# Attention inner loop of a fused transformer kernel: the product with the values split in two halves of queries, and reordered between score products and row maxima

## Chip, core and metric

The kernel runs on one NeuronCore of a Trainium2 chip. The metric is the device time of one launch in microseconds (us): lower is better. The engines have short names here: PE is TensorE's matmul stream, PEld its weight loads, DVE is VectorE, ACT is ScalarE, POOL is GpSimd, SP is SyncE, which issues DMAs.

## What is computed

Four blocks in a row, each followed by a residual sum and a layer norm: a linear state-space scan, a mixture of eight experts with the top two taken, a multi-head attention and a feed-forward block with fp4-style rounding. Only the attention is touched. It runs over 4 sequences of 1024 tokens, 16 heads of 16 channels:

```
qkv = (zn @ W_qkv + b_qkv).reshape(b, n, 3, H, DH)
scores = jnp.einsum('bhqd,bhkd->bhqk', q, k) * scale
attn = jax.nn.softmax(scores, axis=-1)
msa = jnp.einsum('bhqk,bhkd->bhqd', attn, v)
...
out = msa_cat @ W_proj + b_proj
```

## The kernel before

The order of the work is written out by hand for each engine, and engines meet through counting semaphores, which the code calls flows. `F["ex"].wait(pe, b, n)` makes PE wait until flow `ex` has counted n in sequence b. An engine takes its instructions in order, so whatever is behind a waiting one waits too.

Heads are worked in pairs, p = 0 to 7, two heads (a = 0 and 1) at once: head 0 of the pair lies in rows 0 to 49 of `Qs` and `Ks`, head 1 in rows 64 to 113. Each pair has two kinds of score product.

- **Row maxima** (`score_max`, line 925; DVE line 1418). To find the largest score of each query, PE makes 32 products a pair, "units", of 128 queries by 512 keys, alternately of head 0 and head 1, each into a PSUM bank of its own. In the main loop there are three such banks (4, 5 and 6), used in turn, so a unit may start once DVE has reduced the unit three before it (flow `sld`). One DVE instruction reduces one unit.
- **Transposed scores** (`transposed_scores`, line 955). The same scores with keys in the partitions, and with the negated maximum added as two more rows (50 rows instead of 48). Two products, one for each head, give 128 keys by 512 queries. ACT takes the exponential of both in one instruction (line 676) from banks 0 and 1, or 2 and 3, into the buffer `Pb`.

The values are then weighed (`weigh`, line 968): for each head and half of the queries one product of 128 keys, 32 columns of V (16 channels and a column of ones for the softmax sum) and 512 queries, each into 32 partitions of bank 7. The four go to four groups of 32 columns of the array, and run side by side. These operands are plain fp32, and one such product is two MATMUL instructions in the trace, each with a load of its own.

The main loop goes over 64 steps m for each sequence. Step m has the transposed scores of pair p = m // 8 and key tile kt = m % 8, for both halves of the queries (qh = 0, 1), the weighing of step m - 1, and four units of the pair ahead: they run 12 units (three steps) ahead of the pair (`LEAD = 12`), so the last 11 steps of a sequence have none. The units of a pair done, DVE negates the maxima (lines 1422 to 1424, "negation" below), PE turns them (line 932) in the next step, DVE copies them (line 1431), and POOL issues four DMAs (line 497), one behind the other, that bring them into the two extra rows of `Qs`. PE waits for these (flow `mrow`) ahead of the first transposed score of the pair. When a pair is weighed, ACT copies bank 7 out (`evac_o`, line 643); PE waits for that copy (flow `ov`) before it weighs the first tile of the next pair.

Of the kernel before, what the change touches and what calls it, by code (L numbers as in the profile page):

```python
# [14 lines left out]
P = 128  # L15
B, S, D = 4, 1024, 256
N = 16
TT = S // P
DC = D // P
HALF = 512  # L20
NH = S // HALF
E, HID = 8, 512
HC = HID // P
HEADS, DH = 16, 16
NP = HEADS // 2
NB = 4
CH = P // DH
KT = S // P
# [51 lines left out]
def transformer(nc, xT, state_cols, WtT, WbT, Wc4, WoT, Dv, bo, sel, Wg, W1, b1, W2, b2, rev,  # L80
                lnw_d, lnb_d, Wqkv, bqkv_d, Wproj, bproj, w_gate, w_up, w_down, ident_d, out):
    ctx = ExitStack()
    with ctx:
# [150 lines left out]
        def h_dram(name, shape):  # L234
# [25 lines left out]
            ve=1, rs=2, nm=1, vel=2, rsl=4, nml=2, zn=TT, xn=1, xw=TT, xa=TT - 2 + TT // 2, xd=2 + TT // 2, x2=1, vm=1, trp=4 + 2, xt=4 + 2, xl=TT - 3,  # L260
            qkp=8, qka=8, qkv=8, vp=TT, vv=TT, **{f"stk{k}": NP // NB * STK for k in range(NB)}, mrow=16 * 4 * NP,
            slp=SLOTS, sld=SLOTS, nms=NP,
            bp=2 * KT * NP, ex=2 * KT * NP, pv=KT * NP, ov=NP,
            op=TT // 2, on=TT, mp=TT, mt=TT, pr=TT, rr=TT,
            xq=2, xr=2, px=8, xm=2, xp=2, gup=TT, sg=TT, hh=TT, hq=TT, htp=TT, htv=TT, dp=TT, dr=TT,
            outd=16, xfree=1, ahead=0, chain=0,
# [278 lines left out]
        def _(act):  # L545
# [93 lines left out]
            def sequence(b, more):  # L639
                def evac_o(p):  # L640

                    F["pv"].wait(act, b, KT * (p + 1))
                    F["ov"].inc(act.activation(OP[:, p, :], PS[:, 7, :], ACT.Copy))

                def late_norm(i):
# [23 lines left out]
                for p in range(NP):  # L669
                    for kt in range(KT):  # L670
                        for qh in range(2):
                            n = 2 * (KT * p + kt) + qh
                            F["bp"].wait(act, b, n + 1)
                            if n >= 4:
                                F["pv"].wait(act, b, (n - 4) // 2 + 1)
                            F["ex"].inc(act.activation(Pb[:, kt % 2, 2 * qh:2 * qh + 2, :],  # L676
                                                       PS[:, 2 * qh:2 * qh + 2, :], ACT.Exp, scale=0.25))
                        if kt == 0 and p > 0:
                            evac_o(p - 1)
                evac_o(NP - 1)  # L680
                if more:
                    ahead_root(b, 1)
# [60 lines left out]
        def _(pe):  # L743
# [135 lines left out]
            with pe.Fori(0, B) as b:  # L879
# [13 lines left out]
                for u in range(8):  # L893
                    c, w, th = u // 4, (u % 4) // 2, u % 2
                    if u >= 4:
                        F["qkv"].wait(pe, b, u - 3)
                    for kc in range(DC):
                        if w:
                            tokens = XT[:, kc, th * HALF:(th + 1) * HALF].rearrange("p (i q) -> p i q", q=P)
                        else:  # L900
                            tokens = XT[:, kc, :].rearrange("p (i h q) -> p h i q", h=2, q=P)[:, th, :, :]
                        ins = pe.matmul(PS[:, u % 4, :].rearrange("p (i q) -> p i q", q=P),  # L902
                                        wqkv[:, kc, w * D + c * P:w * D + (c + 1) * P], tokens,
                                        start=(kc == 0), stop=(kc == DC - 1))
                    F["qkp"].inc(ins)
                def values(t):
# [30 lines left out]
                def maxima(upto):  # L937

                    while issued[0] < min(upto, NP * UN):
                        n = issued[0]  # L940
                        if n >= UN + 4 and n % UN == 4:
                            turn_max(n // UN - 1)
                        score_max(n)
                        issued[0] += 1
                        if issued[0] == NP * UN:
                            turn_max(NP - 1)

                def transposed_scores(p, kt, qh):

                    n = 2 * (KT * p + kt) + qh  # L950
                    if n >= 2:
                        F["ex"].wait(pe, b, n - 1)
                    for a in range(2):
                        rows = slice(ROW * a, ROW * a + MROWS)
                        ins = pe.matmul(PS[:, 2 * qh + a, :], Ks[rows, p % NB, kt * P:(kt + 1) * P],  # L955
                                        Qs[rows, p % NB, qh * HALF:(qh + 1) * HALF], start=True, stop=True)
                    F["bp"].inc(ins)

                def weigh(m):

                    p, kt = m // KT, m % KT
                    if kt == 0 and p:
                        F["ov"].wait(pe, b, p)
                    F["ex"].wait(pe, b, 2 * m + 2)
                    for qh in range(2):
                        for a in range(2):
                            j = 2 * a + qh
                            ins = pe.matmul(PS[32 * j:32 * j + 32, 7, :], V[:, kt, 2 * p + a, :], Pb[:, kt % 2, 2 * qh + a, :],  # L968
                                            start=(kt == 0), stop=(kt == KT - 1), skip_group_check=True)
                    F["pv"].inc(ins)  # L970

                values(0)
# [8 lines left out]
                for m in range(NP * KT):  # L981
                    p, kt = m // KT, m % KT
                    if kt == 0:
                        F["mrow"].wait(pe, b, 16 * 4 * (p + 1))
                    ahead = UN + LEAD + 4 * m
                    transposed_scores(p, kt, 0)
                    maxima(ahead + 2)
                    transposed_scores(p, kt, 1)
                    maxima(ahead + 3)
                    if m:  # L990
                        weigh(m - 1)
                    maxima(ahead + 4)
                weigh(NP * KT - 1)

                F["ov"].wait(pe, b, NP)

# [607 lines left out]
```

How the kernel before makes its waits and increments, by code:

```python
    def wait(self, eng, b, n, ahead=0):  # L62
        eng.wait_ge(self.sem, b * self.per + (ahead * self.per + n))
# [12 lines left out]
    def wait(self, eng, n):  # L76
        eng.wait_ge(self.sem, n)
# [255 lines left out]
        @block.sync  # L333
# [62 lines left out]
                e_now = e_next  # L396
                if k >= 2:
                    store_y(k - 2)
                if k in (1, 4, 7):
                    for q in range(2):
                        C[f"mid{q}"].wait(sp, 16 * B // 2)
                    load_ffn(k // 3, (w_gate, w_up, w_down)[k // 3])
            store_y(TILES - 2)
            store_y(TILES - 1)
            sp.wait_ge(s_wev, len(turns))
            sp.wait_ge(s_one, 1)
            for k in range(NB):
                for a in range(2):
# [17 lines left out]
                                at = ROW * a + row * DH  # L427
                                F[f"stk{k}"].inc(sp.dma_start(dst[at:at + DH, k, :].bitcast(F32), lo if part else hi), by=16)
                F["xa"].wait(sp, b, TT - 2 + TT // 2)
                F["xd"].wait(sp, b, 2 + TT // 2)
                hold(sp, "sp")
                F["outd"].inc(sp.dma_start(out.rearrange("(n p) d -> p n d", p=P)[:, bass.ds(b * TT, TT), :],
                                           X[:, :, :]), by=16)
                F["outd"].wait(sp, b, 16)
                sp.sem_inc(F["xfree"].sem, 1)
                F["xfree"].seen += 1
            sp.wait_ge(F["outd"].sem, 16 * B)
# [2 lines left out]
        @block.gpsimd  # L440
# [98 lines left out]
                sequence(b, True)  # L539
            sequence(B - 1, False)
            pool.wait_ge(s_one, 1 + 16 * 2 * NB)
```

## Time and profile before

| | |
|---|---|
| time, median of 3 runs | 1864.62 us (1864.11 to 1867.95) |
| the profiled execution: its own time | 1860.18 us |
| its span, from first to last instruction | 1858.5 us |
| mean clock granted to TensorE, as a share of 2.4 GHz | 0.912 |
| PE, PEld, DVE, ACT, POOL busy | 87%, 50%, 69%, 44%, 17% of the span |

The three times are of other executions than the profiled one, which was 4.4 us below their median. Busy shares are means over stages with different limits, and PE is counted busy while its pipeline is full, so 87% does not say that PE is at its peak. Main loops of the attention fill four stretches of some 190 us each, from about 520, 865, 1210 and 1555 us.

### The profile page before, as it was taken

The numbers are of one execution on the slowest core, as the hardware profiler recorded it, in microseconds if no ns is written. First come the engines' busy times: TensorE is split into PE (matmuls) and PEld (weight loads), VectorE is DVE, ScalarE is ACT, GpSimd is POOL, SyncE is SP. The second block draws the span as 40 slices with busy tenths as digits, with TensorE's granted clock in tenths as the row PEclk, the third lists the DMA queues.
The fourth block names the chain that finished last, engine by engine and source line by source line (L and its number), as shares of the span: only waits on it lengthen the run. The fifth ranks groups of instructions, "written<-read, shape, count | busy, mean of one in ns | idle before, by whom it ended". The sixth has DMA issues, their size and how long they took to land.

```text
span 1858.5 us, 25769 instructions
## 1 busy us (share of the span) xinstructions
PE 1614.6 (87%) x7834; PEld 924.4 (50%) x7834; DVE 1275.2 (69%) x2551; ACT 825.5 (44%) x1255; POOL 307.6 (17%) x367
## 2 busy tenths in 40 slices
PE   5969999993899996979999788899986988999786
PEld 2758888883443324644333356433334744333354
DVE  3672322212689977958998687788968958997586
ACT  1302233230357773342776624266772333776522
POOL 0243222213000222000004030100323000000020
PEclk8989999997779998996999989789998987999898
DMA  3227867763312200022222000412200031210000
GB/s 127 68 68 226 263 227 226 233 213 119 65 22 36 64 24 1 1 46 48 36 36 70 1 1 2 92 19 36 64 25 1 1 63 32 40 30 1 1 1 23
DMA packets 86203, 123.08 MB, mean 66 GB/s; under 512 B 16474, under 2 KB 62811, under 8 KB 86059
## 3 DMA queue, kind: packets, MB, share of 16 engines
q1 hardware_dynamic: 74058, 97.92, 20.2%
q0 software_dynamic: 12000, 23.35, 4.4%
q8 instruction: 77, 1.26, 0.3%
q14 instruction: 68, 0.55, 0.1%
HBM read 76.84 MB, written 18.61 MB: 51 GB/s over the span
## 4 chain that ended last, share of the span: by engine, by line
PE 65%; DVE 19%; issue 6%; ACT 3%; DMA 3%; POOL 2%; SPq 1%; DVEq 0%; ACTq 0%; POOLq 0%
PE PS L925 12%; PE PS L968 11%; DVE MX L1418 10%; PE PS L845 7%; PE PS L857 7%; PE PS L1050 6%; PE PS L1060 5%; PE PS L955 2%; PE PS L911 2%; PE PS L796 2%; DMA Qs<-MR 2%; ACT Pb L676 1%; PE PS L1011 1%; PE PS L1080 1%; PE PS L902 1%
## 5 line engine op out<-in xcount | busy, mean ns | idle before, releaser
L1418 DVE TENSOR_REDUCE MX<-PS 128x1 f32<-128x512 f32 x1024 | 636.3, 681 | 86.9 <-PE PS L925 86.1
L676 ACT ACTIVATE Pb<-PS 128x1024 f32<-128x1024 f32 x512 | 498.4, 1023 | 200.5 <-PE PS L955 199.8
L925 PE MATMUL PS<-Ks,Qs 48*128 48x512 f32 x1024 | 389.6, 496 | 43.3 <-DVE MX L1418 12.4
L925 PEld LDWEIGHTS PS<-Ks,Qs 48*128 48x128 f32 x1024 | 177.4, 203 | 362.0 <-DVE MX L1418 324.1
L955 PE MATMUL PS<-Qs,Ks 50*128 50x512 f32 x1024 | 308.8, 450 | 12.3 <-DMA Qs<-MR 7.5
L968 PE MATMUL PS<-Pb,V 128*32 128x512 f32 x2048 | 281.7, 623 | 2.7 <-ACT Pb L676 2.7
L955 PEld LDWEIGHTS PS<-Qs,Ks 50*128 50x128 f32 x1024 | 144.8, 192 | 64.2 <-ACT Pb L676 51.5
L497 POOL DMA_DIRECT2D Qs<-MR x128 | 66.0, 523 | 652.3 <-DVE MR L1431 375.7
L1318 DVE TENSOR_TENSOR V<-PS,V 128x512 f32<-128x512 f32 x39 | 26.9, 691 | 203.1 <-PE PS L857 203.1
L857 PE MATMUL PS<-Pb,OT 128*128 128x256 f32 x624 | 141.0, 379 | 0.0
L603 ACT ACTIVATE OT<-PS,b1t 128x256 f32<-128x256 f32 x156 | 65.5, 471 | 158.7 <-PE PS L845 158.7
L857 PEld LDWEIGHTS PS<-Pb,OT 128*128 128x128 f32 x624 | 115.7, 190 | 14.2
L1050 PE MATMUL PS<-wgT,XT 128*128 128x352 f32 x256 | 101.6, 550 | 15.3 <-DVE OT L1516 12.3
L458 POOL DMA_INDIRECT OT<-x_mid,idx x78 | 74.3, 952 | 217.8 <-PE PS L835 179.4
L1060 PE MATMUL PS<-wdT,Pb 128*128 128x256 f32 (+1 forms) x384 | 101.9, 410 | 8.0 <-ACT Pb L725 8.0
L1060 PEld LDWEIGHTS PS<-wdT,Pb 128*128 128x128 f32 (+1 forms) x384 | 74.3, 202 | 34.6 <-issue 10.6
L1050 PE MATMUL PS<-wuT,XT 128*128 128x352 f32 x256 | 81.6, 462 | 0.0
L1050 PEld LDWEIGHTS PS<-wgT,XT 128*128 128x128 f32 x256 | 56.4, 232 | 46.9 <-issue 15.2
L968 PEld LDWEIGHTS PS<-Pb,V 128*32 128x32 f32 x2048 | 40.8, 109 | 74.9 <-issue 64.9
L845 PE MATMUL PS<-OT,Pb 128*128 128x256 f32 x320 | 75.4, 390 | 0.7 <-ACT OT L594 0.7
L705 ACT ACTIVATE OT<-PS 128x704 f32<-128x704 f32 x32 | 24.2, 756 | 105.4 <-PE PS L1050 105.4
L845 PE MATMUL PS<-V,Pb 128*128 128x256 f32 x304 | 69.0, 380 | 1.0 <-ACT V L594 1.0
(278 smaller groups left out, 1861.7 us busy)
## 6 DMA issues: line engine op xcount, KB each, us to landing
Pb<-W SPq DMA_DIRECT2D x78, 512.0 KB, 3.8
y_slot<-V SPq DMA_DIRECT2D x39, 256.0 KB, 3.8
Qs<-Qh SPq DMA_DIRECT2D x128, 64.0 KB, 2.3
Ks<-Kh SPq DMA_DIRECT2D x128, 64.0 KB, 2.3
V<-b SPq DMA_DIRECT2D x39, 128.0 KB, 3.6
XT<-x_mid POOLq DMA_DIRECT2D x4, 1024.0 KB, 6.3
out<-X SPq DMA_DIRECT2D x4, 1024.0 KB, 4.6
OT<-xT SPq DMA_DIRECT2D x2, 1024.0 KB, 6.3
```

The costliest lines, as they stand in the source:

```text
L458: C[("xa", "xb", "xc")[k % 3]].inc(pool.indirect_dma_start(Xm[k % 3][:, a, :], None, x_mid[:, :], bass.IndirectOffsetOnAxis(idx[:, SA * k ...
L497: F["mrow"].inc(pool.dma_start(Qs[r:r + 1, p % NB, :].rearrange("o (t q) -> o t q", t=TT).bitcast(F32), MR[at:at + TT, p % 2, :].bitcast(F ...
L603: C["hr"].inc(act.activation(HTm[k % 2][:, hc, :], PS[:, 2 + 2 * (k % 2) + hc // 2, hc % 2 * ST:(hc % 2 + 1) * ST], ACT.Relu, bias=b1t[:, ...
L676: F["ex"].inc(act.activation(Pb[:, kt % 2, 2 * qh:2 * qh + 2, :], PS[:, 2 * qh:2 * qh + 2, :], ACT.Exp, scale=0.25))
L845: ins = pe.matmul(PS[:, 2 + 2 * (k % 2) + hc // 2, hc % 2 * ST:(hc % 2 + 1) * ST], W1t[k % 2][:, c, hc * P:(hc + 1) * P], XTm[k % 2][:, c, :],
L857: ins = pe.matmul(PS[:, 6 + k % 2, a * D:(a + 1) * D], HTm[k % 2][:, hc, a * P:(a + 1) * P], W2t[k % 2][:, hc, :], start=(hc == 0), stop=( ...
L925: F["slp"].inc(pe.matmul(PS[:, slot_bank(i), :], Qs[rows, p % NB, t * P:(t + 1) * P], Ks[rows, p % NB, kh * HALF:(kh + 1) * HALF], start=T ...
L955: ins = pe.matmul(PS[:, 2 * qh + a, :], Ks[rows, p % NB, kt * P:(kt + 1) * P], Qs[rows, p % NB, qh * HALF:(qh + 1) * HALF], start=True, st ...
L968: ins = pe.matmul(PS[32 * j:32 * j + 32, 7, :], V[:, kt, 2 * p + a, :], Pb[:, kt % 2, 2 * qh + a, :], start=(kt == 0), stop=(kt == KT - 1) ...
L1050: ins = pe.matmul(PS[:, 2 * w + a, 0:IH], XT[:, c, t * P:(t + 1) * P], wT[:, c, a * IH:(a + 1) * IH], start=(c == 0), stop=(c == DC - 1))
L1060: ins = pe.matmul(PS[:, 6 + t % 2, 0:D], HT[0:k, c, :], wdT[0:k, c, :], start=(c == 0), stop=(c == IC - 1))
L1418: F["sld"].inc(dve.tensor_reduce(MX[:, p % 2, a, t, kh:kh + 1], PS[:, slot_bank(i), :], AX.X, ALU.max))
```

## The change

1. `weigh(m)` becomes `weigh(m, qh)`. Each call weighs one half of the queries that the two transposed score products of that half have made, and that one ACT instruction has exponentiated. It waits for that exponential alone instead of both. So that all four column groups stay in use, the half is cut in two quarters c of 256 queries (`QW`): four products of 256 queries instead of four of 512. There are two calls a step. Flow `pv` counts halves now.
2. The order in a step is, for each half: one unit, two transposed score products (head 1 first), one unit, the weighing of that half of step m - 1. Before, it was: two transposed, two units, two transposed, one unit, whole weighing, one unit.
3. On ACT, the exponential waits for the weighing half that read its buffer (`n - 3` of halves; before, the whole step), and `evac_o` moves from behind the second exponential of a pair's first step to between the first and the second.
4. The queries are laid out in another order in `Qh`, by an access pattern of four dimensions in the Q projection (line 902), so that the results lie where they lay. The number and size of these products stay.

```diff
-                    F["pv"].wait(act, b, KT * (p + 1))
+                    F["pv"].wait(act, b, 2 * KT * (p + 1))
...
                             if n >= 4:
-                                F["pv"].wait(act, b, (n - 4) // 2 + 1)
+                                F["pv"].wait(act, b, n - 3)
                             F["ex"].inc(act.activation(Pb[:, kt % 2, 2 * qh:2 * qh + 2, :],
                                                        PS[:, 2 * qh:2 * qh + 2, :], ACT.Exp, scale=0.25))
-                        if kt == 0 and p > 0:
-                            evac_o(p - 1)
+                            if kt == 0 and p > 0 and qh == 0:
+                                evac_o(p - 1)
...
-                            tokens = XT[:, kc, :].rearrange("p (i h q) -> p h i q", h=2, q=P)[:, th, :, :]
+                            tokens = XT[:, kc, :].rearrange("p (h i c q) -> p h c i q", h=2, i=2, c=2, q=P)[:, th, :, :, :]
...
-                    for a in range(2):
+                    for a in (1, 0):
...
-                def weigh(m):
+                def weigh(m, qh):
...
-                    F["ex"].wait(pe, b, 2 * m + 2)
-                    for qh in range(2):
+                    F["ex"].wait(pe, b, 2 * m + qh + 1)
+                    for c in range(2):
                         for a in range(2):
-                            j = 2 * a + qh
-                            ins = pe.matmul(PS[32 * j:32 * j + 32, 7, :], V[:, kt, 2 * p + a, :], Pb[:, kt % 2, 2 * qh + a, :],
-                                            start=(kt == 0), stop=(kt == KT - 1), skip_group_check=True)
+                            j = 2 * a + c
+                            ins = pe.matmul(PS[32 * j:32 * j + 32, 7, qh * QW:(qh + 1) * QW], V[:, kt, 2 * p + a, :],
+                                            Pb[:, kt % 2, 2 * qh + a, c * QW:(c + 1) * QW],
+                                            start=(kt == 0 and qh == 0), stop=(kt == KT - 1), skip_group_check=True)
...
-                    transposed_scores(p, kt, 0)
-                    maxima(ahead + 2)
-                    transposed_scores(p, kt, 1)
-                    maxima(ahead + 3)
-                    if m:
-                        weigh(m - 1)
-                    maxima(ahead + 4)
-                weigh(NP * KT - 1)
+                    for qh in range(2):
+                        maxima(ahead + 2 * qh + 1)
+                        transposed_scores(p, kt, qh)
+                        maxima(ahead + 2 * qh + 2)
+                        if m:
+                            weigh(m - 1, qh)
+                for qh in range(2):
+                    weigh(NP * KT - 1, qh)
```

On PE, this is one step of the main loop before (`PS<-Qs,Ks` are the transposed scores, `PS<-Ks,Qs` the units, `PS<-Pb,V` the weighing; the brackets name the flow waited for, and a REGISTER_ALU works out the count to wait for):

```order
L955 MATMUL PS<-Qs,Ks 128x512 [waits f_ex]
L955 MATMUL PS<-Qs,Ks 128x512
L63 REGISTER_ALU
L925 MATMUL PS<-Ks,Qs 128x512 [waits f_sld]
L63 REGISTER_ALU
L925 MATMUL PS<-Ks,Qs 128x512 [waits f_sld]
L63 REGISTER_ALU
...
L925 MATMUL PS<-Ks,Qs 128x512 [waits f_sld]
L968 MATMUL PS<-Pb,V 32x512 [waits f_ex]
L968 MATMUL PS<-Pb,V 32x512 x3
L63 REGISTER_ALU
L925 MATMUL PS<-Ks,Qs 128x512 [waits f_sld]
```

And this is half a step of the changed kernel, up to the unit that begins the next half:

```order
L927 MATMUL PS<-Ks,Qs 128x512 [waits f_sld]
L64 REGISTER_ALU
L957 MATMUL PS<-Qs,Ks 128x512 [waits f_ex]
L957 MATMUL PS<-Qs,Ks 128x512
L64 REGISTER_ALU
L927 MATMUL PS<-Ks,Qs 128x512 [waits f_sld]
L970 MATMUL PS<-Pb,V 32x256 [waits f_ex]
L970 MATMUL PS<-Pb,V 32x256 x3
L64 REGISTER_ALU
L927 MATMUL PS<-Ks,Qs 128x512 [waits f_sld]
```

Between two units there now stands either a group of two transposed products or a weighing half, never a whole weighing; a step has two switches into the weighing and two out of it where it had one and one.

On ACT, this is the first step of a pair before (`Pb<-PS` is the exponential, `OT<-PS` the copy of bank 7):

```order
L676 ACTIVATE Pb<-PS 128x1024 [waits f_pv]
L63 REGISTER_ALU
L676 ACTIVATE Pb<-PS 128x1024 [waits f_pv,f_bp]
L63 REGISTER_ALU
L643 ACTIVATE OT<-PS 128x512 [waits f_pv]
L63 REGISTER_ALU
L676 ACTIVATE Pb<-PS 128x1024 [waits f_pv,f_bp]
```

And the same step in the changed kernel:

```order
L677 ACTIVATE Pb<-PS 128x1024 [waits f_pv,f_bp]
L64 REGISTER_ALU
L677 ACTIVATE Pb<-PS 128x1024 [waits f_pv,f_bp]
L644 ACTIVATE OT<-PS 128x512 [waits f_pv]
L64 REGISTER_ALU
L677 ACTIVATE Pb<-PS 128x1024 [waits f_pv,f_bp]
```

The row ahead of the copy is the first exponential of the step now, and the row behind it the second; the copy still waits for the last weighing of the pair, which PE issues after the transposed scores of that second exponential.

## Rows read from the trace of the kernel before

**Rows 1.** The page, part 4: the chain that ended last, by line.

```profile
PE PS L925 12%; PE PS L968 11%; DVE MX L1418 10%; PE PS L845 7%; PE PS L857 7%; PE PS L1050 6%; PE PS L1060 5%; PE PS L955 2%; PE PS L911 2%; PE PS L796 2%; DMA Qs<-MR 2%; ACT Pb L676 1%; PE PS L1011 1%; PE PS L1080 1%; PE PS L902 1%
```

**Rows 2.** Negation to negation: us, busy us of PE, PEld, DVE, ACT, POOL, granted clock.

```profile
584.16:606.44 22.28, 21.36 (x129) 8.15 (x121) 20.51 (x36) 15.98 (x17) 2.00 (x4) 1.00 0.23 37
```

**Rows 3.** DVE's maxima, 584.16 to 606.44 us: busy us, mean ns, idle before.

```profile
L1418 DVE TENSOR_REDUCE MX<-PS 128x1 f32<-128x512 f32 x32 | 19.9, 682 | 1.7 <-PE PS L925 1.7
```

**Rows 4.** Timeline of one step: start, length, engine, line, count, idle time before.

```profile
1008.76 0.49 PE L925 MATMUL PS<-Ks,Qs 48*128 48x512 f32 x1
1008.76 0.72 PE L955 MATMUL PS<-Qs,Ks 50*128 50x512 f32 x2
1009.09 0.63 PE L925 MATMUL PS<-Ks,Qs 48*128 48x512 f32 x2
1009.29 2.48 DVE L1418 TENSOR_REDUCE MX<-PS 128x1 f32<-128x512 f32 x4 [0.22 <-PE PS L925]
1009.33 0.63 PE L955 MATMUL PS<-Qs,Ks 50*128 50x512 f32 x2
1009.60 1.94 ACT L676 ACTIVATE Pb<-PS 128x1024 f32<-128x1024 f32 x2 [0.79 <-PE PS L955]
1010.03 0.49 PE L925 MATMUL PS<-Ks,Qs 48*128 48x512 f32 x1
1010.45 1.06 PE L968 MATMUL PS<-Pb,V 128*32 128x512 f32 x8
1011.45 0.49 PE L925 MATMUL PS<-Ks,Qs 48*128 48x512 f32 x1
...
1011.98 0.69 DVE L1418 TENSOR_REDUCE MX<-PS 128x1 f32<-128x512 f32 x1 [0.21 <-PE PS L925]
```

**Rows 5.** Timeline of a pair's first step, after its wait for the maxima's DMA.

```profile
1003.93 0.50 PE L955 MATMUL PS<-Qs,Ks 50*128 50x512 f32 x2 [0.96 <-DMA Qs<-MR]
...
1004.72 0.40 PE L925 MATMUL PS<-Ks,Qs 48*128 48x512 f32 x1
1005.05 0.16 PEld L968 LDWEIGHTS PS<-Pb,V 128*32 128x32 f32 x8 [0.37 <-issue]
...
1006.37 0.60 ACT L643 ACTIVATE OT<-PS 128x512 f32<-128x512 f32 x1
...
1006.85 1.96 ACT L676 ACTIVATE Pb<-PS 128x1024 f32<-128x1024 f32 x2
```

**Rows 6.** Timeline from a pair's copied maxima to its first transposed scores.

```profile
608.94 0.27 DVE L1431 CAST MR<-PS 32x128 fp32r<-32x128 f32 x1
...
609.88 1.99 POOL L497 DMA_DIRECT2D Qs<-MR x4 [20.37 <-DVE MX L1418]
...
613.51 0.50 PE L955 MATMUL PS<-Qs,Ks 50*128 50x512 f32 x1
```

**Rows 7.** Line 497, all its DMAs: who waited for them; time to landing.

```profile
PE PS L955: 7.5, 9
...
DMA to landing us min/median/max: 1.6/1.6/3.4
```

**Rows 8.** Timeline, PE: products of 256 columns on the whole array, first layers.

```profile
225.83 3.62 PE L857 MATMUL PS<-Pb,OT 128*128 128x256 f32 x16
229.28 2.97 PE L845 MATMUL PS<-OT,Pb 128*128 128x256 f32 x13
```

**Rows 9.** Timeline, PE, in the last steps of a sequence, which have no units.

```profile
1026.98 1.06 PE L968 MATMUL PS<-Pb,V 128*32 128x512 f32 x8
...
1028.88 1.06 PE L968 MATMUL PS<-Pb,V 128*32 128x512 f32 x8
...
1030.72 0.50 PE L955 MATMUL PS<-Qs,Ks 50*128 50x512 f32 x2 [0.34 <-ACT Pb L676]
1031.15 0.64 PE L968 MATMUL PS<-Pb,V 128*32 128x512 f32 x4
```

**Rows 10.** Timeline, prologue: a long run of small products, 78 columns each.

```profile
118.43 3.69 PE L825 MATMUL PS<-Kh,OT 128*128 128x78 f32 x32
```

More of the change, by code:

```diff
@@ L20 @@
 HALF = 512
+QW = HALF // 2
 NH = S // HALF
@@ L262, in transformer @@
             slp=SLOTS, sld=SLOTS, nms=NP,
-            bp=2 * KT * NP, ex=2 * KT * NP, pv=KT * NP, ov=NP,
+            bp=2 * KT * NP, ex=2 * KT * NP, pv=2 * KT * NP, ov=NP,
             op=TT // 2, on=TT, mp=TT, mt=TT, pr=TT, rr=TT,
@@ L900, in _ @@
                         else:
-                            tokens = XT[:, kc, :].rearrange("p (i h q) -> p h i q", h=2, q=P)[:, th, :, :]
-                        ins = pe.matmul(PS[:, u % 4, :].rearrange("p (i q) -> p i q", q=P),
-                                        wqkv[:, kc, w * D + c * P:w * D + (c + 1) * P], tokens,
+                            tokens = XT[:, kc, :].rearrange("p (h i c q) -> p h c i q", h=2, i=2, c=2, q=P)[:, th, :, :, :]
+                        o = PS[:, u % 4, :].rearrange("p (i q) -> p i q", q=P) if w else \
+                            PS[:, u % 4, :].rearrange("p (c i q) -> p c i q", c=2, q=P)
+                        ins = pe.matmul(o, wqkv[:, kc, w * D + c * P:w * D + (c + 1) * P], tokens,
                                         start=(kc == 0), stop=(kc == DC - 1))
```

## The prediction

> **What bounds it now.** I read the page first. Its chain puts 12%, 11% and 10% of the span on the units, the weighing and DVE's maxima, and 2% on the transposed scores: the attention's main loop is where the change can act [rows 1]. I next cut this loop from one negation of the maxima to the next, which is eight steps. It takes 22.28 us at a granted clock of 1.00, so the clock explains nothing here [rows 2]. PE is busy 21.36 us of it and DVE 20.51: both look full, and neither is. DVE is idle 1.7 us, all of it waiting for units [rows 3].
>
> The timeline says who waits for whom [rows 4]. From one step to the next (1008.76 to 1011.45) it is 2.69 us. Follow one cycle. DVE begins a reduction at 1009.29; it takes 0.68 [rows 3], and its bank is free at 1009.97. The unit for that bank starts at 1010.03, alone, since it came late. 0.42 later, at 1010.45, the weighing starts; 1.00 later, at 1011.45, the next unit, and 0.53 later, at 1011.98, DVE reduces it, after 0.21 idle. 0.68 + 0.06 + 0.42 + 1.00 + 0.53 = 2.69: that is the period. DVE itself needs less: four reductions follow each other in 2.48, so (2.48 - 0.68) / 3 = 0.60 each, 2.40 a step. PE also needs less: its products of two heads run two at a time, groups start 0.33 apart after a switch (1008.76, 1009.09) and 0.24 apart after that (two of 0.39 in 0.63). Four groups and the weighing would be 0.33 + 2 x 0.24 + 0.33 + 1.00 = 2.14. So the loop is bound by a ring of waits, in which the long weighing stands between two units.
>
> **The change, part by part.** *The ring.* A weighing half takes the place of the whole between two units. What does it cost? Products of 256 columns follow each other in (229.28 - 225.83) / 16 = 0.216 us [rows 8]. The weighing is two rounds of four products side by side; at 512 columns the rounds would be 2 x 0.43 = 0.86, and 1.00 is measured, so 0.14 is fill, load and switch. A half is then 2 x 0.216 + 0.14 = 0.57. No row shows it. Its bounds: 0.50 if everything halves, 1.00 if nothing does; I take 0.57, because the rows of 256 columns bear it out. The ring is then at most 0.68 + 0.06 + 0.42 + 0.57 + 0.53 = 2.26 for four reductions, under DVE's 2.40. It no longer binds.
>
> *PE's own work* grows, since it pays the switch twice. Per half: first group 0.33, then from the second group to the weighing 0.33 (1004.72 to 1005.05, a group that came in time) [rows 5], then 0.57: 1.23, so 2.47 a step in place of 2.14. The number of units and transposed products stays, and in the new order each still has one of the other head beside it (unit of head 0 with scores of head 1, scores of head 0 with unit of head 1). So PE at 2.47 becomes the limit, DVE at 2.40 right behind it. The Trainium skill (TensorEngine Tiling (Array Packing), Tiling Modes, Key Properties) says that a change of tiling mode drains TensorE, which speaks against this change. The timeline agrees, and has the drain with a price: 0.33 into the weighing where 0.24 is the plain spacing. By the page the doubled switches would cost a drain of which it gives no size there; the sum above goes by the rows.
>
> *The copy of bank 7* (`evac_o`) now stands ahead of a pair's second exponential, and waits for the last weighing half of the pair before, which PE issues behind the second transposed scores. Count from the start of a pair's first step. Second scores start at 1.23; weighing half at 1.23 + 0.66 = 1.90, ended some 0.62 later, at 2.52; the copy goes from 2.58 and holds ACT 0.48 (1006.37 to 1006.85) [rows 5], to 3.06. Then the exponential, 1.02 (two in 1.94, 0.92 apart) [rows 4], to 4.08. The second scores of the next step write its banks and would start at 2.47 + 1.23 = 3.70; they start at 4.14. That is 0.44 lost once a pair, with the units and the weighing behind them in PE's queue, and DVE behind these. Bounds: 0 if something else is late anyway, 0.6 with the copy in full.
>
> *Negation and turn.* Before, 22.28 - 8 x 2.69 = 0.76 us a pair goes to them. DVE's part of it stays, and DVE has next to no slack now: I keep 0.76.
>
> *The DMAs of the maxima.* From DVE's copy (608.94) to the pair's first scores (613.51) is 4.57 us; the last of four DMAs is issued some 1.5 after 609.88 and lands 1.6 later, at 613.0, so 0.5 early [rows 6, 7]. Two steps lie between; they shrink by 0.45, which leaves 0.1: no wait where nothing disturbs, up to 0.1 a pair otherwise. But nine times in the trace PE does wait, 7.5 us in all, for landings that took up to 3.4 [rows 7]. There the two steps give nothing: 9 x 0.45 = 4 us of gain lost.
>
> *The last steps of a sequence* have no units. They take 1.90 and 2.27 (1026.98, 1028.88, 1031.15), with waits for ACT [rows 9]; PE needs 2 x (0.42 + 0.57) = 1.98 now. I put them at nothing. The Q projection has the same products, flow `pv` only twice the counts: nothing, and for neither is there cover needed.
>
> **Sum.** Per pair 8 x 2.47 + 0.76 + 0.44 = 20.93 instead of 22.28, 1.35 less. There are 7 such stretches in each of 4 sequences: 28 x 1.35 = 38. Less 4 for the late landings: 34. On the profiled execution's 1860.2 that gives 1826; the median of the runs shown lies 4.4 higher, so 1830.
>
> **Rivals.** *A. As summed*, 1815 to 1845: 58%.
>
> *B. DVE is the only bound.* Half weighings come out cheaper, and the copy's 0.44 falls into time that PE has anyway. Then a pair takes what DVE needs: 32 x 0.60 + 0.8 = 20.0, 2.2 less, 28 x 2.2 = 62, less 4: about 1806. For it: DVE is at 20.51 of 22.28 already. Against: by the rows PE needs 2.47 to DVE's 2.40. 10%.
>
> *C. The half is dearer than 0.57.* The margin is thin: with 0.44 lost at the copy, the gain is gone when a step takes 2.69 - 0.44 / 8 = 2.64, that is at a half of 0.66. At 0.63 a step is 2.59, a pair 21.92, the gain 0.36 x 28 = 10, less 4: about 1858, and 1846 to 1861 as its span. For it: the overhead might be per round and per load, and there are as many rounds as before at half the length. Against: two rounds show 0.14 in all. 13%, and 6% that it comes out within 0.2%, which is also the case that the ring was not what held the loop.
>
> *D. Slower: PE's instruction issue becomes the bound.* A step now has 24 products and 24 loads instead of 16 and 16, beside 6 register instructions. It decides from 2.64 / 54 = 49 ns an instruction. For it: the longest run of small products starts one every 3.69 / 32 = 0.115 us, nowhere does a long run go faster, and if that is issue, it is some 56 ns for each of product and load [rows 10]. Then a step is at least 24 x 0.112 = 2.69: 28 x 0.44 = 12 slower, 1877, and 54 x 0.056 = 3.02 if register instructions cost as much: 28 x 3.1 = 87 slower, 1952. Against: from a standing start at 1003.93, PE had the seven products that the program puts ahead of the weighing, with their loads, and the eight loads of the weighing itself behind it by 1005.21, with five register instructions: 27 in 1.28 us, 47 ns at most, though products filled that time [rows 5]. And the run of small products has loads of 128 columns, which may be what sets its pace. 13%.
>
> The Trainium skill (TensorE: Matmul & The Clock Gate, "Wait — 56ns, not 53.3ns?") has a rule for this rival: with hardware decode off, the sequencer spends about 62 ns on each matmul. By that, an estimate, 24 matmuls take 1.49 us of a step, which hides; with loads at the same price it would be 2.98, and the change a loss. No row here tells which decode is on.
>
> **Numbers.** A and B and most of C are faster by over 0.2% (about 3.7 us, what a measurement can tell from no change): 58 + 10 + 13 = 81%. Same 6%, slower 13%. The forecast is A's 1830. The range for 8 in 10 leaves out half of B below 1806 and D above 1860, so 1806 to 1860; A's own is 1815 to 1845.
>
> **What the profile after would show.** Ring gone: the time from negation to negation falls from 22.28 to some 20.9, and DVE's waits for units in it from 1.7 us to under 1. Half weighing: eight products, next group 0.57 after their start. PE bound: groups 0.33, 0.33, 0.57, with no idle time between. The copy: once a pair, transposed scores that wait for ACT, 0.44. Landings: still nine or more waits, of like length. It would be wrong if the half takes 0.66 or more, if loads or products of the weighing start one after the other instead of together, or if idle time of PE ends by "issue" in each step.

## The result and the profile after

The change makes the kernel slower: a median of 1923.80 us (1914.31 to 1947.64, 4 runs) against 1866.28 us for the kernel before beside it, a ratio of 1.029 (95% interval 1.025 to 1.033). 1830 was predicted, with 1806 to 1860 as the range.

The stretch on which the prediction was built did get faster. This is one half step of the changed kernel in its timeline, in the columns of [rows 4] (line 927 is a unit, 957 the transposed scores, 970 the weighing), and the unit that begins the next half:

```profile
1007.29 0.50 PE L927 MATMUL PS<-Ks,Qs 48*128 48x512 f32 x1
...
1007.29 0.73 PE L957 MATMUL PS<-Qs,Ks 50*128 50x512 f32 x2
...
1007.63 0.40 PE L927 MATMUL PS<-Ks,Qs 48*128 48x512 f32 x1
...
1007.96 0.64 PE L970 MATMUL PS<-Pb,V 128*32 128x256 f32 x8
...
1008.53 0.50 PE L927 MATMUL PS<-Ks,Qs 48*128 48x512 f32 x1
```

The groups start 0.34, 0.33 and 0.57 us apart, 1.24 in all, where 1.23 was forecast. From one negation to the next (the last instruction of each) it is 21.25 us instead of 22.28 [rows 2]:

```profile
607.33 0.18 DVE L1427 TENSOR_TENSOR NMs<-NM,NMs 128x16 fp32r<-128x16 f32 x1
...
628.58 0.17 DVE L1427 TENSOR_TENSOR NMs<-NM,NMs 128x16 fp32r<-128x16 f32 x1
```

The groups of instructions in a stretch of that length, 593.35 to 614.61, show where the idle time went (busy us, mean ns, idle before):

```profile
L1421 DVE TENSOR_REDUCE MX<-PS 128x1 f32<-128x512 f32 x34 | 21.3, 685 | 0.6 <-PE PS L927 0.5
...
L927 PE MATMUL PS<-Ks,Qs 48*128 48x512 f32 x32 | 12.5, 453 | 0.0
L957 PE MATMUL PS<-Qs,Ks 50*128 50x512 f32 x32 | 11.4, 450 | 0.0
L970 PE MATMUL PS<-Pb,V 128*32 128x256 f32 x132 | 10.6, 391 | 0.0
```

DVE's waits fell from 1.7 us [rows 3] to 0.6, and PE has none. The ring is gone.

The loss is in other steps, and it has one name. Here are two windows views, before and after, of the second sequence, each cut into steps 0 to 7, 8 to 52 and 53 to 63 (the columns are those of [rows 2]: length, busy time of PE, PEld, DVE, ACT and POOL, then the granted clock, and last the DMA share and GB/s). Before:

```profile
866.60:891.50 24.90, 23.48 (x124) 9.71 (x124) 22.10 (x39) 15.84 (x16) 2.05 (x4) 0.87 0.04 7
891.50:1019.10 127.60, 121.17 (x728) 46.69 (x728) 115.69 (x203) 90.94 (x96) 27.03 (x39) 1.00 0.24 50
1019.10:1043.30 24.20, 22.32 (x141) 6.06 (x140) 13.95 (x43) 21.30 (x23) 2.11 (x4) 0.93 0.01 2
```

After, the second sequence and, ahead of it, the middle of the first:

```profile
550.30:672.10 121.80, 119.28 (x1090) 44.60 (x1086) 116.94 (x206) 94.47 (x97) 26.76 (x39) 1.00 0.25 54
...
881.40:914.50 33.10, 33.10 (x179) 11.71 (x178) 22.27 (x38) 16.28 (x16) 2.06 (x4) 0.50 0.01 2
914.50:1043.50 129.00, 126.17 (x1090) 46.35 (x1086) 116.75 (x205) 94.14 (x97) 27.10 (x39) 0.93 0.24 51
1043.50:1082.10 38.60, 38.60 (x240) 11.24 (x236) 13.59 (x42) 22.91 (x23) 2.12 (x4) 0.51 0.01 1
```

In the second sequence after, the granted clock is 0.50, 1.2 GHz, for all of the first eight steps and nearly all of the last eleven, and PE is busy without a gap in both. The low clock also reaches into the middle stretch (0.93). Where it doesn't (first sequence), the middle takes 121.8 instead of 127.5 us. Over the four sequences:

| us in the profiled executions | before | after | difference |
|---|---|---|---|
| steps 0 to 7 | 25.6 + 24.9 + 24.7 + 25.1 = 100.3 | 27.7 + 33.1 + 33.1 + 33.1 = 127.0 | +26.7 |
| steps 8 to 52 | 127.5 + 127.6 + 130.3 + 128.8 = 514.2 | 121.8 + 129.0 + 131.3 + 123.8 = 505.9 | -8.3 |
| steps 53 to 63 | 24.4 + 24.2 + 23.4 + 24.0 = 96.0 | 39.3 + 38.6 + 39.4 + 39.3 = 156.6 | +60.6 |
| the rest of the span | 1148.0 | 1156.5 | +8.5 |

The profiled execution took 1947.64 us, 24 above the median; in the other three the mean granted clock was 0.858 to 0.868 instead of 0.845, so part of the table's sum of 87.5 us is its own.

In the last steps the timeline reads, with the exponential beside it:

```profile
692.93 0.79 PE L957 MATMUL PS<-Qs,Ks 50*128 50x512 f32 x2
693.65 0.20 PEld L970 LDWEIGHTS PS<-Pb,V 128*32 128x32 f32 x8 [0.44 <-issue]
693.66 1.08 PE L970 MATMUL PS<-Pb,V 128*32 128x256 f32 x8
693.77 1.02 ACT L677 ACTIVATE Pb<-PS 128x1024 f32<-128x1024 f32 x1 [0.71 <-PE PS L957]
694.66 0.29 PEld L957 LDWEIGHTS PS<-Qs,Ks 50*128 50x128 f32 x2 [0.81 <-issue]
```

A half is 0.73 + 1.00 = 1.73 us, 3.46 a step, with ACT waiting 0.71 a half. At 2.4 GHz it would be 1.98 by the prediction's own sum, close to what ACT's two exponentials take there (four in 3.79 us before, at 1028.70, so 1.90 a step).

What PE did before the clock fell: it waited 1.85 us for the last negation, at the end of step 52.

```profile
1042.74 0.28 PE L934 MATMUL PS<-ident,NMs 128*32 128x128 f32 x1 [1.85 <-DVE NMs L1427]
```

The kernel before has such a wait at the same place, of 1.50 us, in each sequence, and in three of the four the clock falls behind it too. But there it is back after 3.4 us:

```profile
1020.00:1023.40 3.40, 3.40 (x16) 0.71 (x12) 3.40 (x11) 2.66 (x4) 2.11 (x4) 0.51 0.06 10
1023.40:1043.30 19.90, 18.02 (x124) 4.93 (x116) 9.81 (x32) 18.32 (x20) 0.00 (x0) 1.00 0.00 1
```

The same holds at the start of a sequence: both kernels enter it at 1.2 GHz. In the second sequence the clock is up 6.6 us into the loop before, and 50.1 us into it after. In seven of these eight places the clock is low before too, for 3 to 11 us. With the change it is up again much later, at the start after 20 to 50 us, at the end not within the loop.

### The profile page after: what moved, and what is told of

The parts are those of the page before. It is cut to its first block, busy times and chain, and to the rows that moved or that the text cites. A ratio compares the mean times of both kernels' runs of the same rounds, so it can differ in the third digit from the quotient of the medians.

```text
span 1946.0 us, 29873 instructions
## 1 busy us (share of the span) xinstructions
PE 1726.8 (89%) x9882; PEld 951.0 (49%) x9882; DVE 1280.7 (66%) x2551; ACT 845.9 (43%) x1255; POOL 308.5 (16%) x367
## 4 chain that ended last, share of the span: by engine, by line
PE 76%; DVE 12%; issue 5%; ACT 3%; DMA 2%; SPq 1%; POOL 1%; DVEq 0%; ACTq 0%; POOLq 0%
PE PS L970 17%; PE PS L927 12%; PE PS L957 8%; PE PS L846 7%; PE PS L858 7%; PE PS L1053 6%; PE PS L1063 4%; DVE MX L1421 4%; PE PS L913 2%; PE PS L797 1%; PE PS L1014 1%; PE PS L1083 1%; SPq L429 1%; PE PS L836 1%; PE PS L1004 1%
## 5 line engine op out<-in xcount | busy, mean ns | idle before, releaser
L677 ACT ACTIVATE Pb<-PS 128x1024 f32<-128x1024 f32 x512 | 519.2, 1026 | 231.2 <-PE PS L957 230.9
L927 PE MATMUL PS<-Ks,Qs 48*128 48x512 f32 x1024 | 427.8, 528 | 28.1 <-DVE MX L1421 10.9
L957 PE MATMUL PS<-Qs,Ks 50*128 50x512 f32 x1024 | 409.5, 546 | 0.0
L970 PE MATMUL PS<-Pb,V 128*32 128x256 f32 x4096 | 396.9, 468 | 1.1
L957 PEld LDWEIGHTS PS<-Qs,Ks 50*128 50x128 f32 x1024 | 160.1, 220 | 73.5 <-issue 66.9
L970 PEld LDWEIGHTS PS<-Pb,V 128*32 128x32 f32 x4096 | 88.8, 118 | 210.9 <-issue 106.3
L1471 DVE RECIPROCAL rc<-PS 128x16 f32<-128x16 f32 x32 | 7.9, 248 | 120.6 <-PE PS L1004 119.9
```

The lines of the kernel that those rows point to most:

```text
L927: F["slp"].inc(pe.matmul(PS[:, slot_bank(i), :], Qs[rows, p % NB, t * P:(t + 1) * P], Ks[rows, p % NB, kh * HALF:(kh + 1) * HALF], start=T ...
L970: ins = pe.matmul(PS[32 * j:32 * j + 32, 7, qh * QW:(qh + 1) * QW], V[:, kt, 2 * p + a, :], Pb[:, kt % 2, 2 * qh + a, c * QW:(c + 1) * QW] ...
```

## Experiments

Two theories at first. Theory 1: the order of the work, with the two halves apart, holds the clock at 1.2 GHz where there is little between them. Theory 2: the products of 256 columns do so, in whatever order. "The old order" below is that of the kernel before, with both halves of a step back to back at its place for the weighing. It takes the place of these lines of the changed kernel, in all steps or, under a condition on m, in some, while the others keep the changed order. `(0, 1)` puts head 0 first, as before:

```diff
-                    for qh in range(2):
-                        maxima(ahead + 2 * qh + 1)
-                        transposed_scores(p, kt, qh)
-                        maxima(ahead + 2 * qh + 2)
-                        if m:
-                            weigh(m - 1, qh)
+                    transposed_scores(p, kt, 0, (0, 1))
+                    maxima(ahead + 2)
+                    transposed_scores(p, kt, 1, (0, 1))
+                    maxima(ahead + 3)
+                    if m:
+                        weigh(m - 1, 0)
+                        weigh(m - 1, 1)
+                    maxima(ahead + 4)
```

### Halves in the old order, in all steps (split_old_order)

> Weighing in two halves of queries as in the changed kernel, but back to back, and units, transposed scores and weighing in the order of the kernel before. Theory 1 (the order of the work keeps the granted clock at 1.2 GHz in the first and last steps of a sequence): clock as before, last stretch (steps 53 to 63) 24 us a sequence, ring of waits at 2.69 us a step as before, some 1866 us. Theory 2 (products of 256 columns keep the clock down, in whatever order): last stretch near 39 us and first eight steps 28 to 33 us a sequence, 1930 us or more.

Measured: 1883.10 us, ratio 1.007 (1.004 to 1.009). The windows view of its second sequence, cut in the same places:

```profile
874.60:899.90 25.30, 24.89 (x177) 12.66 (x177) 21.05 (x38) 15.80 (x16) 2.04 (x4) 0.75 0.02 4
899.90:1031.80 131.90, 122.08 (x1093) 58.27 (x1089) 117.31 (x205) 90.77 (x97) 27.02 (x39) 1.00 0.23 50
1031.80:1055.40 23.60, 21.23 (x237) 8.97 (x236) 13.95 (x43) 21.30 (x23) 2.11 (x4) 1.00 0.01 2
```

The clock is about that of before (0.913 over the whole execution, 0.912 before), and the last stretch takes 23.6 us. Products of 256 columns, and twice as many instructions and loads, don't keep the clock down: theory 2 falls. The time is 17 us over the 1866 forecast. That is the middle, 4.3 us longer than before (131.9 to 127.6) in this sequence: steps of 3.37 us instead of 2.70 stand twice in each pair there (962.13 to 965.50 and 970.92 to 974.29), at the negation, as before, and at the pair's first step, where ACT's copy now stands between the exponentials.

### The new order of units alone (order_whole)

The kernel before, its weighing whole and of 512 columns, at the end of the step, and head 1 first as in the changed kernel:

```diff
-                    for a in range(2):
+                    for a in (1, 0):
...
-                    transposed_scores(p, kt, 0)
-                    maxima(ahead + 2)
-                    transposed_scores(p, kt, 1)
-                    maxima(ahead + 3)
-                    if m:
-                        weigh(m - 1)
-                    maxima(ahead + 4)
+                    for qh in range(2):
+                        maxima(ahead + 2 * qh + 1)
+                        transposed_scores(p, kt, qh)
+                        maxima(ahead + 2 * qh + 2)
+                    if m:
+                        weigh(m - 1)
```

> The kernel before with units on either side of the transposed scores of each half, and the whole weighing of 512 columns at the end of the step. Theory 1 (order): low clock in the first and last steps, last stretch well over 24 us a sequence, 1900 us or more. Theory 2 (columns): clock as before, a step at 2.69 us since the whole weighing still stands between two units, 1866 us give or take 6.

Measured: 1863.84 us, ratio 0.998 (0.996 to 1.000). Second sequence:

```profile
867.70:891.60 23.90, 23.04 (x124) 9.86 (x123) 21.31 (x38) 15.66 (x16) 2.05 (x4) 0.84 0.02 4
891.60:1018.50 126.90, 119.45 (x732) 46.73 (x728) 117.13 (x207) 90.87 (x97) 27.00 (x39) 1.00 0.24 51
1018.50:1043.20 24.70, 22.41 (x140) 6.21 (x140) 13.10 (x41) 21.30 (x23) 2.11 (x4) 0.93 0.01 2
```

The order of units and scores alone doesn't lower the clock either, so theory 1 falls as it was put. It also gives nothing in the middle: the ring needs the split. What is left is the two halves standing apart, which needs both edits.

### Halves apart, units in the old order (apart_old_units)

The changed kernel, with head 0 first again and this core:

```diff
-                    for qh in range(2):
-                        maxima(ahead + 2 * qh + 1)
-                        transposed_scores(p, kt, qh)
-                        maxima(ahead + 2 * qh + 2)
-                        if m:
-                            weigh(m - 1, qh)
+                    transposed_scores(p, kt, 0)
+                    maxima(ahead + 2)
+                    if m:
+                        weigh(m - 1, 0)
+                    transposed_scores(p, kt, 1)
+                    maxima(ahead + 3)
+                    if m:
+                        weigh(m - 1, 1)
+                    maxima(ahead + 4)
```

> Two weighing halves apart, but units and transposed scores in the order of before: first transposed, two units, first half, second transposed, one unit, second half, one unit. Theory 1a (four switches a step between scores and weighing are what keeps the clock at 1.2 GHz): as in the changed kernel, clock low for most of the first eight steps and all of the last stretch (39 us), 1920 us. Theory 1b (a unit of one head beside the scores of the other is what does it): clock up as in the kernel before at the start of a sequence, by 15 to 20 us after its first scores.

Measured: 2340.15 us, ratio 1.252 (1.248 to 1.257). Theory 1a said 1920, and the time is far longer. Second sequence:

```profile
988.10:1024.70 36.60, 36.60 (x178) 13.98 (x179) 22.33 (x38) 16.39 (x16) 2.05 (x4) 0.50 0.02 3
1024.70:1244.50 219.80, 218.30 (x1091) 78.90 (x1087) 121.83 (x204) 94.45 (x96) 27.04 (x39) 0.50 0.14 30
1244.50:1283.90 39.40, 39.40 (x237) 11.47 (x236) 13.94 (x43) 22.93 (x23) 2.11 (x4) 0.50 0.01 1
```

The clock stays at 1.2 GHz through the whole loop, in all four sequences, with PE busy 218.30 of 219.80 us. Halves apart bring the low clock in this order of the units too. The clock is not all of the 2340 us: a step takes 219.80 / 45 = 4.88 us here, and two halves of the changed order at 1.2 GHz 2 x 2.16 = 4.32 (925.30 to 927.46 in the timeline after), since in this order some units have no product of the other head beside them.

That PE cannot leave 1.2 GHz with the halves apart would be too much said. In the changed kernel it did so in all four sequences, 19.8, 50.1, 50.3 and 37.3 us into the loop, with no gap and no other order before the rise, and the same order then kept 2.4 GHz to the end of its units. The second sequence:

```profile
881.40:931.50 50.10, 50.10 (x274) 17.30 (x273) 32.35 (x54) 24.57 (x25) 2.06 (x4) 0.50 0.10 17
931.50:1043.50 112.00, 109.17 (x994) 40.76 (x990) 106.67 (x190) 85.84 (x88) 27.10 (x39) 1.00 0.23 52
```

So with the halves apart a low clock lasts long, but not without end. What brings it up is not shown.

### More between the switches (padded_tail)

The changed kernel, and in steps 53 to 63 two more products like a unit's behind each pair of transposed scores, read by nobody:

```diff
+                        if m >= 53:
+                            if not padded:
+                                F["sld"].wait(pe, b, SLOTS)
+                            padded.append(1)
+                            for a in range(2):
+                                rows = slice(ROW * a, ROW * a + STACK)
+                                pe.matmul(PS[:, 4 + a, :], Qs[rows, p % NB, kt * P:(kt + 1) * P],
+                                          Ks[rows, p % NB, qh * HALF:(qh + 1) * HALF], start=True, stop=True)
```

> The changed kernel with two more products, like those of the row maxima and read by nobody, behind each pair of transposed scores in steps 53 to 63. Theory 1 (so many switches into and out of the weighing, with little between them, let the clock fall): it stays up for part or all of the last stretch, which takes 27 to 33 us a sequence instead of 39 although it does more, so 25 to 45 us less than the changed kernel. Rival (the low clock is due to something else, and added work is only added): two groups more a step at 1.2 GHz, 11 x 0.9 = 10 us a sequence more, 1960 us.

Measured: 1906.78 us (1888.38 to 1924.38), ratio 1.023 (1.017 to 1.030): some 17 us less than the changed kernel, where the rival had 36 more and the theory 25 to 45 less. The intervals of the two ratios overlap (1.017 to 1.030, and 1.025 to 1.033), so it is the stretches themselves that decide. The last one of each sequence, in the profiled execution (1888.38 us):

```profile
680.60:716.30 35.70, 35.36 (x283) 12.40 (x280) 13.59 (x42) 22.81 (x23) 2.11 (x4) 0.76 0.01 1
1031.70:1061.50 29.80, 29.48 (x284) 10.73 (x280) 13.55 (x42) 22.82 (x23) 2.11 (x4) 0.94 0.01 2
1385.40:1417.40 32.00, 31.68 (x280) 11.43 (x280) 13.12 (x41) 22.80 (x23) 2.11 (x4) 0.87 0.01 2
1733.40:1761.80 28.40, 28.08 (x284) 10.46 (x280) 2.49 (x8) 22.81 (x23) 2.06 (x4) 1.00 0.01 2
```

With 44 more products a sequence the stretch is 3 to 11 us shorter than 39, and it is the shorter the higher its clock. Work that is only added can't do that: what the stretch gains is clock. The forecast of 27 to 33 us holds for three of the four.

### The old order where the clock is lost (old_tail, old_head, old_head_tail)

The changed kernel, with `if m >= 53`, `if m < 8`, and `if m < 8 or m >= 53` over the old order.

> The changed kernel with the order of before, and both weighing halves together, in steps 53 to 63 of each sequence alone, which have no units. Theory 1 (order): the last stretch falls from 39 to 24 us a sequence, 4 x 15 = 60 us less than the changed kernel, some 1865 us. Theory 2 (columns): it stays near 39 us, 1920 us.

Measured: 1867.32 us, ratio 0.999 (0.997 to 1.002), as forecast. The last stretch of its second sequence takes 24.50 us at clock 0.93.

> The changed kernel with the old order and both weighing halves together in steps 0 to 7 of each sequence alone; steps 53 to 63 are as changed. If the two low stretches of the clock are separate losses that add up, the last stretch stays at 39 us a sequence and the time is 1841 + 60 = 1900 us. If low clock at the start of a sequence also brings it about at the end, the last stretch falls too, to some 24 us, and the time is near 1841.

Measured: 1897.99 us, ratio 1.015 (1.011 to 1.019). Its second sequence has a middle of 121.90 us at clock 1.00 and still

```profile
1027.60:1066.20 38.60, 38.60 (x240) 11.24 (x236) 13.58 (x42) 22.91 (x23) 2.11 (x4) 0.51 0.01 1
```

so the two losses are separate: even out of a long stretch at 2.4 GHz the clock, once it has fallen behind the wait at step 52, stays down when the halves are apart.

> As the one with the old order in steps 53 to 63, and also in steps 0 to 7. Theory 1: the first eight steps fall to 25 us a sequence and the clock is up at the end of them, so another 7 x 4 = 28 us or more less than with the last steps alone: some 1830 us, which would be the time predicted. Theory 2: no clear change against the changed kernel, 1920 us.

Measured: 1841.12 us (1836.73 to 1858.07), ratio 0.983 (0.980 to 0.987), faster than before, and 11 us over the 1830 forecast. In its first sequence,

```profile
520.70:545.90 25.20, 24.68 (x179) 12.54 (x181) 21.43 (x38) 15.83 (x16) 2.00 (x4) 0.79 0.03 5
545.90:667.70 121.80, 119.36 (x1089) 44.90 (x1085) 116.89 (x206) 93.90 (x96) 26.70 (x39) 1.00 0.25 54
667.70:693.70 26.00, 23.88 (x240) 9.82 (x236) 13.55 (x42) 21.42 (x23) 2.11 (x4) 0.87 0.01 2
```

the first and last stretches are about those of before and the middle has the whole gain. The third sequence of the profiled execution (1858.07 us) didn't keep it: 141.60 us for the middle at clock 0.84.

### What becomes of a pause (early_last_half, old_after_pause, late_copy, and two of them again)

In the third sequence PE waits 1.7 to 2.0 us at the start of step 24, for late DMAs of the maxima, in nearly every kernel here (the expectations call it a pause of 2.4 us). In the kernel before the clock falls behind it for 3.4 us. early_last_half is old_head_tail with both halves of a pair's last weighing in the first half of the next pair's first step; old_after_pause has the old order in steps 24 to 29 too; late_copy is old_head_tail with ACT's copy back behind the second exponential.

```diff
-                            if m:
-                                weigh(m - 1, qh)
+                            if kt:
+                                weigh(m - 1, qh)
+                            elif qh == 0:
+                                weigh(m - 1, 0)
+                                weigh(m - 1, 1)
...
-                    if m < 8 or m >= 53:
+                    if m < 8 or 24 <= m < 30 or m >= 53:
```

> The one with the old order in steps 0 to 7 and 53 to 63, and in each pair's first step both weighing halves in the place of the first. ACT's copy of bank 7 then finds its input done by the time it is issued. If that copy costs 0.44 us a pair, as predicted, the 0.44 goes, and some 0.1 to 0.25 comes back because a whole weighing stands between two units once a pair: 24 to 28 pairs x 0.2 to 0.35 = 5 to 10 us less than 1841 us. If it is absorbed by DVE's lag anyway, no change or some us more.

Measured: 1841.32 us, ratio 0.985 (0.982 to 0.989). Its middle stretch is 120.3 us at clock 1.00 in the first sequence, 1.5 less than in old_head_tail, which is 0.27 in each of 5.6 pairs and so in the forecast of 0.2 to 0.35. The time forecast, 5 to 10 us less than 1841, did not come; two medians of different chips don't resolve so little.

> The one with the old order in steps 0 to 7 and 53 to 63 and the early last half, and with the old order in steps 24 to 29 too. In the third sequence PE pauses 2.4 us for a late DMA at the start of step 24; the clock falls behind it in all kernels, for 3.4 us in the one before and for 24 to 44 us where the new order follows. Theory: with four switches a step the clock doesn't come back, with two it does: low time of that stretch 3 to 7 us again, 10 to 20 us gained there, 4 x 6 x 0.23 = 5.5 us lost for the old order elsewhere: 1828 to 1838 us. Rival (how long it stays low is chance): no gain, 5 us more, 1847 us.

> The one with the old order in steps 0 to 7 and 53 to 63, with ACT's copy of bank 7 behind the second exponential, as in the kernel before. If the copy's place between the exponentials costs 0.44 us a pair, that stall goes, but the next pair's first weighing half, due 3.13 us into the pair, waits for a copy that ends at 3.7: 0.6 us in its place, so 20 to 24 pairs x 0.1 to 0.2 = 2 to 5 us more, 1845 us. Rival (the new place is what costs, and the wait for the copy is hidden): 10 us less, 1831 us.

Measured: 1916.81 us, ratio 1.004 (1.001 to 1.006), and 1911.16 us, ratio 0.999 (0.996 to 1.002). These two ran on a chip on which the kernel before took 1911.30 us, and where PE also paused at steps 41 to 43 and 49 in three sequences; neither time can be set beside the others, and on the place of the copy the run is inconclusive. Behind the pause at step 24 the two profiled executions can be compared. Old order there (old_after_pause):

```profile
1325.00:1331.00 6.00, 4.65 (x28) 2.27 (x28) 2.37 (x4) 1.90 (x3) 0.00 (x0) 0.72 0.53 89
1331.00:1337.00 6.00, 5.22 (x50) 2.69 (x50) 4.98 (x9) 4.57 (x6) 0.00 (x0) 1.00 0.25 40
```

New order there (late_copy):

```profile
1312.00:1318.00 6.00, 4.95 (x32) 1.86 (x36) 3.31 (x6) 2.95 (x4) 0.00 (x0) 0.71 0.52 85
1318.00:1336.00 18.00, 18.00 (x106) 5.73 (x98) 11.40 (x20) 8.90 (x9) 0.00 (x0) 0.50 0.09 15
```

So both kernels were run once more, side by side, on a third chip.

> The same kernel as in the run before, with the old order in steps 24 to 29 too, since the chip of that run paused PE at other steps as well, in the kernel before also. On a chip where the kernel before takes some 1866 us: the low time behind the pause at step 24 of the third sequence is 3 to 7 us, the time 1828 to 1838 us. Rival: no gain over the one without, 1841 to 1847 us.

> The version without the old order in steps 24 to 29, beside it on the same chip. Theory: low for 24 us or more behind the pause at step 24 of the third sequence, 1841 us, 5 to 13 us more than with the old order there. Rival: the same time or less.

Measured: 1842.87 us (1841.06 to 1847.81), ratio 0.985 (0.983 to 0.988), and 1839.90 us (1835.17 to 1852.17), ratio 0.983 (0.980 to 0.986). Behind the pause, with the old order at steps 24 to 29 and without:

```profile
1272.00:1296.00 24.00, 22.72 (x209) 10.49 (x213) 21.43 (x38) 16.78 (x18) 2.05 (x4) 1.00 0.19 32
```

```profile
1269.40:1306.00 36.60, 36.51 (x205) 12.82 (x209) 22.19 (x38) 17.28 (x18) 2.05 (x4) 0.50 0.15 24
```

This does not bear the theory out. The forecast was 3 to 7 us at the low clock behind the pause with the old order there; in that profile the clock did not fall behind the pause, so nothing had to come back. The medians are 3 us apart the other way, and both times are those of the rivals (1841 to 1847, and the same or less). The profiled execution without the old order at step 24 took 1852.17 us, 12 over the median.

An earlier run already spoke against "24 to 44 us where the new order follows". In old_head the changed order follows the same pause (1306.33, after 2.03 us), and the clock is back after 3.2 us, still in that order:

```profile
1308.40:1311.60 3.20, 3.20 (x22) 0.90 (x21) 2.38 (x4) 2.02 (x3) 0.00 (x0) 0.50 0.51 83
1311.60:1330.00 18.40, 18.40 (x175) 6.95 (x173) 17.57 (x32) 14.32 (x15) 2.05 (x4) 1.00 0.08 14
```

Over all profiles, the low time behind the pause at step 24 is 0 (the changed kernel, padded_tail), 3.2, 24 (three runs), 37 and 44 us with the halves apart, and 0, 3.4 (two runs), 6.5 and 9.5 us with them together or whole. Long low stretches occur only with the halves apart, but one profile of each kernel does not say how often; the rival, that chance has a part in their length, stands. The best version is old_head_tail or early_last_half, 1.5 to 1.7% faster than the kernel before.

## Why the prediction was wrong

**What bounds it now.** Right for the stretch that was read: the ring of waits set 2.69 us a step, and it vanished. But this part says "the clock explains nothing here", since the stretch had a granted clock of 1.00. That is the step that failed. It took the clock of one stretch for that of all steps, and as given for the kernel after. The kernel before is at 0.80 to 0.87 in the first eight steps, and at 0.93 in the last eleven of three sequences; the prediction has no row of these clocks and no term for them. The runs showed in its place 127.0 instead of 100.3 us for the first eight steps of the four sequences and 156.6 instead of 96.0 for the last eleven, at 0.50 or near it.

**The half weighing.** Forecast 0.57, measured 0.57, though no row of before showed it. **PE's work** 1.23 a half, measured 1.24. The doubled switches were priced in time (0.33 for 0.24) and this price was right; what halves apart do to the clock had no term. None of the three signs by which the prediction said it would be wrong came (a half of 0.66, products one after the other, PE idle by "issue"): they watched the stretch at 2.4 GHz only.

**The copy of bank 7.** Forecast 0.44 a pair. Around the copy the weighing halves start 1.36 and 1.57 us apart where 1.24 is plain, 0.12 + 0.33 = 0.45:

```profile
1009.20 0.64 PE L970 MATMUL PS<-Pb,V 128*32 128x256 f32 x8
...
1010.56 0.64 PE L970 MATMUL PS<-Pb,V 128*32 128x256 f32 x8
...
1012.13 0.64 PE L970 MATMUL PS<-Pb,V 128*32 128x256 f32 x8
```

The size is right, the path only in part: the first 0.12 is the next pair's first weighing, which waits for the copy itself (its loads, at 1010.55, after 0.49 idle by ACT's line 644), and the forecast has no such wait.

**Negation and turn.** Forecast 0.76. A pair takes 21.24, less 16 x 1.24 and 0.45 leaves 0.95: mis-sized by 0.2. So the gain is 1.04 instead of 1.35 a pair, where the clock is up. The forecast's own terms, 8 x 2.47 + 0.76 + 0.44, make 20.96 and not the 20.93 it has, which changes little.

**Late landings.** At least nine waits were forecast; in the profile after PE waited three times, 2.5 us in all. Why so few was not followed up. The term was 4 us.

**The last steps.** Put at nothing, on PE needing 1.98 us a step at 2.4 GHz. They were the main loss, 60.6 us in the profile, as 3.46 us a step at 1.2 GHz. The number 1.98 was within 0.1 of the 1.90 that ACT takes there, and left PE no idle time in a stretch of scores and weighings alone.

**The sum.** With the clock kept up by the old order at both ends, old_head_tail takes 1841 us, 0.983 of before, where 1830, or 0.981, was predicted for the change as it stands. That these two are so near is in part luck: old_head_tail has the new order in 45 of 64 steps only, and its middle gains 5.7 us in the first sequence (127.5 to 121.8), some 23 in four. The sum stands in its mechanism where the clock is up, and is too large by 0.3 us a pair. The missing term is the clock: 1923.80 against 1841.12, 83 us.

**Rivals.** None of the four was it. D had the right side for another reason, which is luck: its price was 49 ns or more for an instruction, and a half has 27 instructions in 1.24 us, 46 ns each, with no idle time of PE. C was wrong, the half cost what A said.

**The cause.** Shown: the loss is time at 1.2 GHz (windows, padded_tail); neither the halving nor the order alone brings it (split_old_order, order_whole); halves apart do, in either order of units (the changed kernel, apart_old_units); the old order in 19 of 64 steps takes most of it away (old_head_tail). Open: why halves apart keep the clock down, and what ends it where it ends. The middle of apart_old_units has PE busy 218.30 of 219.80 us at 0.50, that of order_whole 119.45 of 126.90 at 1.00. The Trainium skill (TensorE: Matmul & The Clock Gate, Part 1) says that activity of the array releases the throttle; by busy time as a profile shows it, the first of these two should have had the higher clock, and it had the lower. The Trainium skill (TensorEngine Tiling (Array Packing), Tiling Modes, Key Properties), which the prediction cites, says that a change of tiling mode drains TensorE. Whether these drains have a part in the low clock is not shown: no run here changed them and nothing else.

## What to carry over

A sum in TensorE time holds for a clock; ask for each stretch, and above all for those with little else in them, what the change does to it, and read the granted clock there before and after. A change that splits a product and spreads its parts can lose the clock that it would need, with PE busy all the time: here it stayed down for 20 to 50 us at the start of each sequence and for nearly all of the last eleven steps, where the order before had it back in 3 to 11 us. A single profiled execution shows that this happens, not how often. A rearrangement need not be all or nothing: the new order where it pays and the old one at both ends turned 3% slower into 1.7% faster.

## What was unexpected in the hardware

A full PE can stay at 1.2 GHz for as long as its loop lasts: 219.8 us a sequence in apart_old_units, with no idle time to speak of. A PE with waits got 2.4 GHz: in steps 8 to 52 of order_whole it was busy 94% of the time at clock 1.00. And behind one wait of 1.7 to 2.0 us PE had nothing to 9.5 us at the low clock with the weighing together, and anything from nothing to 44 with its halves apart.
